# A decoder block on one core: the experts' tokens in half blocks of 64, two with different weights in one product

## The chip, the cores and the metric

The kernel runs on one core of a Trainium2 chip. The metric is the device time of one execution in microseconds (us), here the median of three runs. TensorE is called PE (PEld is its weight load), VectorE DVE, ScalarE ACT, GpSimd POOL and SyncE SP; a name with a q behind it (SPq, PEldq) is the sequencer of that engine, which issues DMAs and works on registers.

## What is computed

A decoder block with pre-normalisation on 4 x 1024 tokens of width 256: causal linear attention with 16 heads, cross attention to 77 context tokens, and a feed-forward part. The feed-forward part is what the change is in:

```python
x1 = x @ sw1.T + sb1;  x2 = x @ sw2.T + sb2            # shared, every token
sh = ln(silu(x1) * x2, s_ln_g, s_ln_b)
shared_out = sh @ sw3.T + sb3
x_moe = x[index_b, index_t]                            # 512 of the 4096 tokens
top1_idx = argmax(sigmoid(x_moe @ eg_w.T + eg_b) + exp_bias)   # one of 8 experts
weights = softmax([shared_score, top1_score])
h1 = x_moe @ ew1[e].T + eb1[e];  h2 = x_moe @ ew2[e].T + eb2[e]
z = ln(silu(h1) * h2, sel_ln_g, sel_ln_b)
expert_out = z @ ew3[e].T + eb3[e]
out[index_b, index_t] = shared_out * weights[0] + expert_out * weights[1]
```

All three parts are added to their input. Everything is float32.

## The kernel before

A tile is 128 tokens; there are 32. Attention and cross attention run as a software pipeline over the tiles (`step(i)` on each engine). Then comes a pipeline over units, in the order of `UNITS`: six groups of four tiles for the shared feed-forward (F0 to F5), G0 (the 512 gathered tokens, for the shared part and for the choice of experts), F6, F7, and the experts' units M0, M1 and M2. Each engine has a loop over q (from 3 to the number of units, or one more) and does in step q its share of units q - 2 to q + 2: `to_features` transposes a unit's input on PE, `gate_products` makes its two hidden products, `z_features` transposes the hidden values, `y_products` makes the output, `gated` and `y_evict` are DVE's parts, `evict_features` and `evict_z` ACT's. Every engine takes its instructions strictly in the order written, so a unit's place in these loops sets what waits behind what. On PE step q = 8 ends with `y_products(7)` (of F6, unit 7) and `to_features(9)` (of M0, unit 9); step 9 is then `z_features(8)`, `gate_products(9)`, `to_features(10)`, `y_products(8)`; step 10 the first half of `gate_products(10)`, `z_features(9)`, the second half, and so on.

The experts' path works as follows. DVE picks each gathered token's expert and its rank among that expert's tokens (`choose_experts`, `choose_slots`). The tokens of an expert are laid out in blocks of 128 slots, each expert starting a new block; there can be at most 4 + 8 - 1 = 11 blocks (`NBLK`), most of them partly empty. POOL scatters the normalised tokens to their slots in DRAM (line 1761, four indirect DMAs). SP waits for them (`placed`) and loads the blocks back (`hs_in`, line 475, one DMA for each M unit of four blocks, the last of three). PE waits for them in `to_features` (`hs_loaded`). `map_blocks` on DVE finds each block's expert. PE reads that number from SBUF into a register (`load_expert`, line 882), and the register picks the weights `we_12` and `we_3` of a block's products from the tiles that hold all eight experts (lines 753 and 803). The bias comes in by one more product with `block_hot` (lines 755 and 806). Meanwhile POOL scatters the rest of each token's result, its weight and its row number to the same slots (line 1735), and SP loads them as `res` (line 467). After the experts' layer norm (POOL finds one over the square root, `m_r`, line 1672), POOL scatters each block's 128 rows to the output, one indirect DMA for each block (line 1746); rows of empty slots fall outside the bounds. In its step q POOL does `scatter_blocks(q - 2)` first and `invert_blocks(q)` last.

SP's part around the change, in its order: for each unit, in `UNITS` order, `store_out` of an F unit waits for DVE's `y_evict` of that unit and stores it; on reaching G0 it waits for `placed` and issues the loads of `hs_in`; on reaching F7 it issues the first `load_base`.

Of the kernel before, what the change touches and what calls it, by code (L numbers as in the profile page):

```python
# [39 lines left out]
NBLK = MT + NE - 1  # L40
# [21 lines left out]
def decoder_block(nc, A):  # L62
    ctx = ExitStack()
    with ctx:  # L64
# [143 lines left out]
        hs_in = wide_[:, 0:2816].rearrange("p (b d) -> p b d", b=NBLK)  # L208
# [3 lines left out]
        m_th, m_u, m_z = (wide_[:, n:n + 512].rearrange("p (j n) -> p j n", j=GT) for n in (9792, 10304, 10816))  # L212

# [5 lines left out]
        iota12 = sb("iota12", [P, 12])  # L219
        iota128 = sb("iota128", [P, MT])  # L220
        over = sb("over", [P, NE, MT])
# [7 lines left out]
        past = sb("past", [P, NBLK, NE])  # L229
        block_e = sb("block_e", [P, 12])  # L230
        block_i = sb("block_i", [P, 12], I32)
        block_oh = sb("block_oh", [BIAS_ROWS, NBLK, NE])
        block_sum = sb("block_sum", [BIAS_ROWS, 12])
        block_hot = sb("block_hot", [BIAS_ROWS, 12], BF16)
# [80 lines left out]
        scattered = sem("scattered")  # L315

# [22 lines left out]
        def is_tile(t):  # L339
            return 0 <= t < NT  # L340

# [50 lines left out]
        def _(sp):  # L392
# [94 lines left out]
        def _(pe):  # L487
# [242 lines left out]
            def gate_products(pe, n, half, expert=None, load_expert=None):  # L730
# [15 lines left out]
                else:  # L746
                    k = UNITS[n][1]
                    for j in range(2 * half, min(2 * half + 2, size(n))):
                        b = GT * k + j
                        dst = sbank[2 + half][:, (j % 2) * D:(j % 2 + 1) * D]  # L750
                        for ch in range(CH):
                            w = we_12[:, bass.ds(expert[b], 1), ch, :].rearrange("p o n -> p (o n)")
                            pe.matmul(dst, h3t[:, n % 2, ch, j * P:(j + 1) * P], w, start=(ch == 0), stop=False)  # L753

                        mm = pe.matmul(dst, block_hot[:, b:b + 1].to_broadcast([BIAS_ROWS, P]), be_16[:, 0:2 * HF],  # L755
                                       start=False, stop=True)
                        if j + 1 < size(n):
                            load_expert()
# [23 lines left out]
            def y_products(pe, n, expert=None, load_expert=None):  # L782
# [10 lines left out]
                for j in range(size(n)):  # L793

                    if is_moe(n) and j % 2 == 0:
                        wait(pe, ys_ready, GT * UNITS[n][1] - 2 + j)
                    if is_dense(n):
                        w = w_3c[:, :]
                    else:
                        wait(pe, mzt_ready, UNITS[n][1] + 1 + (j >= parts(n)[0][1]))  # L800
                        w = we_3[:, bass.ds(expert[GT * UNITS[n][1] + j], 1), :].rearrange("p o n -> p (o n)")
                    dst = bank[1 + j // 2][:, (j % 2) * D:(j % 2 + 1) * D]
                    mm = pe.matmul(dst, z_t[:, n % 2, j * P:(j + 1) * P], w, start=True, stop=is_dense(n))  # L803
                    if is_moe(n):
                        b = GT * UNITS[n][1] + j
                        mm = pe.matmul(dst, block_hot[:, b:b + 1].to_broadcast([BIAS_ROWS, P]), be_16[:, 2 * HF:2 * HF + D],
                                       start=False, stop=True)
# [71 lines left out]
            def load_expert():  # L879
                b = len(expert)  # L880
                if b < NBLK:
                    expert.append(pe.value_load(block_i[0:1, b:b + 1], min_val=0, max_val=NE - 1))
# [218 lines left out]
        def _(dve):  # L1101
# [258 lines left out]
            def expert_constants():  # L1360
# [4 lines left out]
                dve.tensor_tensor_scan(iota12[:, :], zero1[:, 0:1].to_broadcast([P, 12]),  # L1365
                                       one1[:, 0:1].to_broadcast([P, 12]), -1.0, ALU.add, ALU.add).then_inc(cols_ready, 1)
# [3 lines left out]
                dve.tensor_scalar(iota128[:, :], iota12[:, 0:MT], float(P), None, ALU.mult).then_inc(cols_ready, 1)  # L1370
# [56 lines left out]
            def choose_slots():  # L1427
# [3 lines left out]
                then_wait(dve.tensor_tensor(over[:, :, :], total.unsqueeze(2).to_broadcast([P, NE, MT]),  # L1431
                                            iota128[:, :].unsqueeze(1).to_broadcast([P, NE, MT]), ALU.is_gt))
# [4 lines left out]
                then_wait(dve.tensor_scalar(base[:, :], base[:, :], float(P), float(NT * P - 1), ALU.mult, ALU.add))  # L1437
# [11 lines left out]
            def map_blocks():  # L1449
                then_wait(dve.tensor_tensor(past[:, :, :], iota12[:, 0:NBLK].unsqueeze(2).to_broadcast([P, NBLK, NE]),  # L1450
                                            end_block[:, :].unsqueeze(1).to_broadcast([P, NBLK, NE]), ALU.is_ge))
                then_wait(dve.tensor_reduce(block_e[:, 0:NBLK], past[:, :, :], mybir.AxisListType.X, ALU.add))
                then_wait(dve.tensor_scalar(block_e[:, 0:NBLK], block_e[:, 0:NBLK], float(NE - 1), None, ALU.min))
                then_wait(dve.tensor_copy(block_i[:, 0:NBLK], block_e[:, 0:NBLK]))
                rows = slice(0, BIAS_ROWS)
                then_wait(dve.tensor_tensor(block_oh[:, :, :], iota8[rows, :].unsqueeze(1).to_broadcast([BIAS_ROWS, NBLK, NE]),
# [383 lines left out]
```

## Time and profile before

| | |
|---|---|
| time, median of 3 runs | 381.24 us (380.94 to 381.77) |
| the profiled execution's own time | 381.03 us |
| its span, first to last instruction | 379.1 us |
| PE busy | 360.7 us (95%) |
| PE weight load busy | 261.5 us (69%) |
| DVE busy | 298.8 us (79%) |
| POOL busy | 282.3 us (74%) |
| ACT busy | 164.3 us (43%) |

The share of busy time is over the whole span; the change touches only what runs from about 330 us on. Times of instructions are counted from the start of the span.

### The profile page before, as it was taken

The page shows a single profiled execution, that of the slowest core. Times are in us where ns is not written, and L with a number is a line of the kernel's source. Part 1 is how long each engine was busy: PE and PEld are TensorE (multiplying, and loading weights), DVE is VectorE, ACT ScalarE, POOL GpSimd, SP SyncE. Part 2 cuts the span into 40 slices and gives each one's busy share as a digit, 9 for nine tenths or more (in the row PEclk, how much of TensorE's full clock was granted, in tenths as well). Part 3 has the DMA queues.
Part 4 walks back from the last instruction along what each step waited for, and adds up shares of the span by engine and source line. Part 5 has one row for each costly group of instructions (what it writes and reads, how often), then busy time and mean ns, then how long its engine had stood idle before and what let it go on. Part 6 is the DMA issues. An engine that isn't in the chain of part 4 may idle for free. (4 is left out here: it accounts for less than half of the span.)

```text
span 379.1 us, 10587 instructions
## 1 busy us (share of the span) xinstructions
PE 360.7 (95%) x3483; PEld 261.5 (69%) x3483; DVE 298.8 (79%) x934; ACT 164.3 (43%) x395; POOL 282.3 (74%) x417
## 2 busy tenths in 40 slices
PE   8999999999999999999999999999899989998971
PEld 4566677777777777767777777778676566656751
DVE  2588788898989898888898878886756598799771
ACT  1553553453455356436436524432456445341320
POOL 5338987766777866877867789898888888687385
PEclk9999999999999999999999999999999999999997
DMA  8994891300300120032221012003000223136630
GB/s 256 315 310 94 238 298 22 68 16 16 72 30 16 35 54 16 19 83 90 94 52 37 29 24 65 16 22 80 15 30 28 83 86 111 57 115 216 189 109 13
DMA packets 38076, 33.32 MB, mean 88 GB/s; under 512 B 4425, under 2 KB 37224, under 8 KB 38024
## 3 DMA queue, kind: packets, MB, share of 16 engines
q1 hardware_dynamic: 35016, 28.37, 26.4%
q0 software_dynamic: 1456, 3.37, 3.0%
q10 hardware_dynamic: 1552, 0.92, 0.9%
q8 instruction: 29, 0.48, 0.5%
q14 instruction: 23, 0.19, 0.2%
HBM read 15.58 MB, written 13.78 MB: 77 GB/s over the span
## 5 line engine op out<-in xcount | busy, mean ns | idle before, releaser
L1595 POOL TENSOR_TENSOR s_t<-s_t,causal 128x512 f32<-128x512 f32 x63 | 78.9, 1272 | 15.6 <-ACT s_t L909 15.4
L501 PE MATMUL bank<-h1t,w_qkv 128*128 128x512 f32 x112 | 52.9, 595 | 0.4 <-DVE x L1168 0.3
L1155 DVE TENSOR_TENSOR s_t<-sbank,causal 128x512 f32<-128x512 f32 x65 | 43.5, 671 | 1.1 <-PE sbank L522 1.0
L1587 POOL TENSOR_TENSOR state_wide<-state,own_pair 128x256 f32<-128x256 f32 x28 | 18.9, 675 | 25.5 <-DVE state L1146 24.4
L909 ACT ACTIVATE s_t<-sbank 128x512 f32<-128x512 f32 x63 | 33.7, 587 | 7.8 <-PE sbank L522 7.8
L522 PE MATMUL sbank<-arena 32*128 32x256 f32 x512 | 36.7, 400 | 0.0
L561 PE MATMUL bank<-s_t,vp 128*32 128x128 f32 x1024 | 34.6, 275 | 1.1 <-DVE s_t L1155 0.4
L508 PE MATMUL bank<-w_qkv,h1t 128*128 128x256 f32 x128 | 34.2, 389 | 0.0
L1603 POOL TENSOR_TENSOR rr<-ve,neg_half 128x3 f32<-128x3 f32 x36 | 31.9, 887 | 3.0
L646 PE MATMUL bank<-w_out,attn_t 128*128 128x256 f32 x128 | 33.6, 385 | 0.5 <-DVE attn_t L1236 0.5
L740 PE MATMUL sbank<-h1t,w 128*128 128x512 f32 x72 | 33.0, 596 | 0.5 <-ACT h1t L909 0.5
L1190 DVE BATCH_NORM_STATS2 stats<-x 128x6 f32<-128x256 f32 x87 | 31.6, 412 | 0.0
L1112 DVE TENSOR_SCALAR arena<-bank,b_qk 128x512 f32<-128x512 f32 x28 | 21.0, 751 | 13.1 <-PE bank L501 13.1
L909 ACT ACTIVATE prob_t<-bank 77x128 f32<-77x128 f32 x32 | 8.7, 273 | 50.2 <-PE bank L489 50.2
L561 PEld LDWEIGHTS bank<-s_t,vp 128*32 128x32 f32 x1024 | 26.2, 109 | 6.2 <-issue 2.1
L489 PEld LDWEIGHTS bank<-ident,h 128*128 128x128 f32 x128 | 17.6, 140 | 17.3 <-issue 12.4
L501 PEld LDWEIGHTS bank<-h1t,w_qkv 128*128 128x128 f32 x112 | 19.1, 190 | 14.2 <-issue 13.4
L968 ACT ACTIVATE prob<-sc,nmx 128x77 f32<-128x77 f32 x32 | 11.5, 360 | 37.9 <-DVE nmx L1220 37.9
L1614 POOL TENSOR_TENSOR x<-x,b_out 128x256 f32<-128x256 f32 x32 | 26.0, 813 | 0.0
L522 PEld LDWEIGHTS sbank<-arena 32*128 32x128 f32 x512 | 23.1, 184 | 3.9 <-issue 2.4
L646 PEld LDWEIGHTS bank<-w_out,attn_t 128*128 128x128 f32 x128 | 21.8, 190 | 3.5 <-DVE attn_t L1236 1.5
L489 PE MATMUL bank<-ident,h 128*128 128x128 f32 x128 | 24.2, 272 | 0.0
(215 smaller groups left out, 831.7 us busy)
## 6 DMA issues: line engine op xcount, KB each, us to landing
rden_t<-rden SPq DMA_DIRECT2D x64, 64.0 KB
rows<-x SPq DMA_DIRECT2D x32, 128.0 KB, 1.9
x<-in_x SPq DMA_DIRECT2D x7, 512.0 KB, 7.9
out<-x SPq DMA_DIRECT2D x7, 512.0 KB, 2.9
we<-in_we SPq DMA_DIRECT2D x1, 2048.0 KB
rows<-empty SPq DMA_DIRECT2D x1, 1419.0 KB, 6.4
rows<-empty SPq DMA_DIRECT2D x1, 1408.0 KB, 7.6
xmask<-in_mask POOLq DMA_DIRECT2D x2, 616.0 KB, 10.8
```

What stands on the lines that cost most here:

```text
L489: return pe.transpose(dst, src, ident[:, :])
L501: mm = pe.matmul(dst[:, :], w_qkv[:, ch, cb * P:(cb + 1) * P], h1t[:, g % 3, ch, :], start=(ch == 0), stop=(ch == CH - 1))
L508: mm = pe.matmul(v_place(t), h1t[:, (t // GT) % 3, ch, tok(t)], w_qkv[:, ch, 2 * D:3 * D], start=(ch == 0), stop=(ch == CH - 1))
L522: mm = pe.matmul(both, kt(slot, ch)[rows, tok(t)], qpair(slot, ch)[rows, :, tok(t)], start=True, stop=True)
L561: mm = pe.matmul(bank[3][32 * r:32 * r + 32, ch * P:(ch + 1) * P], v_of, s_t[:, r, 2 * ch + par, :], start=(first and ch + par == 0), stop ...
L646: mm = pe.matmul(bank[0][:, 0:D], attn_t[:, M % 2, ch, :], w_out[:, ch, :], start=(ch == 0), stop=(ch == CH - 1))
L740: mm = pe.matmul(sbank[2 + half][:, :], w_12[:, ch, half * HF:(half + 1) * HF], h3t[:, n % 2, ch, :], start=(ch == 0), stop=(ch == CH - 1))
L909: return act.activation(dst, src, ACT.Copy)
L1155: dve.tensor_tensor(s_t[:, r, :, :], sbank[r][:, :].rearrange("p (s q) -> p s q", s=4), causal[:, :].unsqueeze(1).to_broadcast([P, 4, P]), ...
L1190: last = dve.bn_stats(stats[:, k, :], x[:, t, :])
L1595: pool.tensor_tensor(s_t[:, r, :, :], s_t[:, r, :, :], causal[:, :].unsqueeze(1).to_broadcast([P, 4, P]), ALU.mult)\
L1603: pool.tensor_tensor(rr[:, i, :], ve[:, i, :], neg_half[:, 0:3], ALU.pow).then_inc(rr_ready, 1)
```

## The change

A block of 128 slots becomes two halves of 64 slots. Each expert starts a new half, so there are at most 8 + 8 - 1 = 15 halves, held in 8 blocks, and the M units become two of four blocks each. The two halves of a block can belong to different experts. Every product of a block is split in two, each with 64 output partitions (tokens), one for the even half and one for the odd half. The even half's weights come as before by register from the resident tiles. The odd half's weights are loaded from DRAM to places of their own (`we_odd`, in tiles that are free by then), seven blocks with two DMAs each, whose source address SP takes from the odd half's expert number, read by `value_load`. SP does this on reaching G0, ahead of its wait for `placed`. DVE does the first half of `map_blocks` right after `choose_slots`, one step earlier, and the rest (`block_rows`) where it was; the small tiles of both grow (16 halves in place of 11 blocks). The core of it:

```diff
-NBLK = MT + NE - 1
+HB = P // 2
+NHALF = 2 * MT + NE - 1
+NBLK = -(-NHALF // 2)
 NMG = -(-NBLK // GT)
...
+        we_odd = [w_flat[:, 0:we_size], w_flat[:, we_size:2 * we_size], vp_flat[:, 0:we_size],
+                  vp_flat[:, we_size:2 * we_size], rden_t[:, :, :].rearrange("p j d -> p (j d)")[:, 0:we_size],
+                  wide_[:, 2048:2048 + we_size], wide_[:, 11328:11328 + we_size]]
+        we_odd.append(we_odd[-1])
...
                 if n == GATHERED:
+                    sp.wait_ge(expert_ready, 1)
+                    for m in range(NMG):
+                        for b in odd_of(m):
+                            e = sp.value_load(block_i[0:1, 2 * b + 1:2 * b + 2], min_val=0, max_val=NE - 1)
+                            sp.dma_start(we_odd[b][:, 0:2 * CH * HF].rearrange("p (c n) -> p c n", c=CH),
+                                         A["we_12"][bass.ds(e, 1), :, :].rearrange("o (c p) n -> p (o c) n", p=P))\
+                                .then_inc(we_odd_in[m], 16)
+                            sp.dma_start(we_odd[b][:, 2 * CH * HF:we_size],
+                                         A["we_3"][bass.ds(e, 1), :, :].rearrange("o p n -> p (o n)"))\
+                                .then_inc(we_odd_in[m], 16)
                     sp.wait_ge(placed, 16 * MT)
                     for m in range(NMG):
                         b = blocks_of(m)
...
+                    if half == 0:
+                        pe.wait_ge(we_odd_in[k], 16 * 2 * len(odd_of(k)))
                     for j in range(2 * half, min(2 * half + 2, size(n))):
                         b = GT * k + j
                         dst = sbank[2 + half][:, (j % 2) * D:(j % 2 + 1) * D]
                         for ch in range(CH):
-                            w = we_12[:, bass.ds(expert[b], 1), ch, :].rearrange("p o n -> p (o n)")
-                            pe.matmul(dst, h3t[:, n % 2, ch, j * P:(j + 1) * P], w, start=(ch == 0), stop=False)
-
-                        mm = pe.matmul(dst, block_hot[:, b:b + 1].to_broadcast([BIAS_ROWS, P]), be_16[:, 0:2 * HF],
-                                       start=False, stop=True)
+                            w = (we_12[:, bass.ds(expert[b], 1), ch, :].rearrange("p o n -> p (o n)"),
+                                 we_odd[b][:, 2 * ch * HF:2 * (ch + 1) * HF])
+                            for o in range(2):
+                                at = slice(j * P + o * HB, j * P + (o + 1) * HB)
+                                pe.matmul(dst[o * HB:(o + 1) * HB, :], h3t[:, n % 2, ch, at], w[o], start=(ch == 0),
+                                          stop=False, skip_group_check=True)
+
+                        for o in range(2):
+                            hot = block_hot[:, 2 * b + o:2 * b + o + 1].to_broadcast([BIAS_ROWS, HB])
+                            mm = pe.matmul(dst[o * HB:(o + 1) * HB, :], hot, be_16[:, 0:2 * HF],
+                                           start=False, stop=True, skip_group_check=True)
...
-                then_wait(dve.tensor_copy(block_i[:, 0:NBLK], block_e[:, 0:NBLK]))
+                dve.tensor_copy(block_i[:, :], block_e[:, :]).then_inc(expert_ready, 1)
+
+            def block_rows():
...
                 if q == GATHERED:
                     choose_slots()
+                    map_blocks()
                 if q == GATHERED + 1:
-                    map_blocks()
+                    block_rows()
                     weigh()
```

`y_products` is split in the same way, with `we_3` and the last third of `we_odd`. A pair of loads for one block is 256 KB and 128 KB.

## Rows read from the trace of the kernel before

**Rows 1.** POOL in order of time (start, us, what), from 360 us on

```profile
360.38 1.01 POOL L1672 TENSOR_TENSOR m_r<-m_ve,neg_half 128x4 f32<-128x4 f32 x1
361.57 1.05 POOL L1746 DMA_INDIRECT out<-arena,token_u  x1 [0.18 <-issue]
...
365.48 0.97 POOL L1746 DMA_INDIRECT out<-arena,token_u  x1 [0.30 <-issue]
...
366.80 0.88 POOL L1672 TENSOR_TENSOR m_r<-m_ve,neg_half 128x3 f32<-128x3 f32 x1
367.88 1.09 POOL L1746 DMA_INDIRECT out<-arena,token_u  x1 [0.20 <-issue]
...
375.67 0.97 POOL L1746 DMA_INDIRECT out<-arena,token_u  x1 [0.31 <-issue]
```

**Rows 2.** DVE in order of time, its last output

```profile
371.00 1.27 DVE L1301 SCALAR_TENSOR_TENSOR arena<-bank,arena 128x256 f32<-128x256 f32 x3 [1.52 <-PE bank L806]
```

**Rows 3.** PE in order of time, M0's transposes to M1's last gate product

```profile
343.60 1.04 PE L489 MATMUL sbank<-ident,arena 128*128 128x128 f32 x8
344.48 0.60 PE L489 MATMUL bank<-ident,s_t 128*128 128x128 f32 x4
345.91 1.13 PE L753 MATMUL sbank<-we,h1t 128*128 x4 [0.83 <-ACT h1t L909]
346.98 1.03 PE L753 MATMUL sbank<-we,h1t 128*128 x4
...
347.96 1.03 PE L753 MATMUL sbank<-we,h1t 128*128 x4
...
357.35 0.27 PE L755 MATMUL sbank<-be,block_hot 72*128 72x256 bf16 x1
```

**Rows 4.** SP's queue in order of time, 334 to 340 us

```profile
334.05 0.37 SPq L462 DMA_DIRECT2D out<-x  x1
339.46 0.92 SPq L475 DMA_DIRECT2D arena<-rows  x2
```

**Rows 5.** The three loads of hs_in (line 475), issue to landing

```profile
DMA to landing us min/median/max: 3.8/4.9/5.4
```

**Rows 6.** DVE in order of time: F5's output, then map_blocks from first to block_i

```profile
332.37 1.65 DVE L1294 SCALAR_TENSOR_TENSOR x<-bank,z_r,x 128x256 f32<-128x256 f32 x4
...
336.46 0.21 DVE L1450 TENSOR_TENSOR past<-iota,end_block 128x88 f32<-128x88 f32 x1
...
337.19 0.17 DVE L1454 CAST block_i<-block_e 128x11 int32<-128x11 f32 x1
```

**Rows 7.** Reading an expert's number, two in a row, 341 to 342.8 us

```profile
L882 PEldq TENSOR_LOAD <-block_i x2: 299/302/304, 341.3 to 342.0; - x2
L882 PEldq FUSED_REGOPS  x2: 146/146/146, 341.7 to 342.4; - x2
```

**Rows 8.** The page's GB/s by slice; SP's issues in time, and by tile (ns min/median/max)

```profile
GB/s 256 315 310 94 238 298 22 68 16 16 72 30 16 35 54 16 19 83 90 94 52 37 29 24 65 16 22 80 15 30 28 83 86 111 57 115 216 189 109 13
...
0.73 0.46 SPq L394 DMA_DIRECT2D arena<-in_w_xk  x1
...
14.71 4.71 SPq L394 DMA_DIRECT2D x<-in_x  x5
...
L458 SPq DMA_DIRECT2D rows<-x x1: 320/320/320, 55.7 to 55.7; - x1
```

**Rows 9.** PE in order of time in the attention's pipeline, products with 32 columns

```profile
204.47 1.08 PE L561 MATMUL bank<-s_t,vp 128*32 128x128 f32 x32
```

**Rows 10.** Windows: length, busy of PE PEld DVE ACT POOL, granted clock, DMA share, GB/s

```profile
373.00:375.00 2.00, 0.00 (x0) 0.00 (x0) 0.00 (x0) 0.00 (x0) 1.58 (x2) 0.98 0.03 1
375.00:379.10 4.10, 0.00 (x0) 0.00 (x0) 0.00 (x0) 0.00 (x0) 1.33 (x2) 0.50 0.02 0
```

**Rows 11.** PE's first products: in order of time; those in 6 to 8 us, ns min/median/max

```profile
0.99 5.80 PE L843 MATMUL sbank<-ones 128*128 128x512 bf16 x14 [0.99 <-POOL ones L1696]
...
L843 PE MATMUL sbank<-ones x3: 381/484/634, 5.7 to 6.4; 128*128 128x512 bf16 x3
```

More of the change, by code:

```diff
@@ L207, in decoder_block @@
         wide_ = arena[:, :, :].rearrange("p s n -> p (s n)")
-        hs_in = wide_[:, 0:2816].rearrange("p (b d) -> p b d", b=NBLK)
+        hs_in = wide_[:, 0:2048].rearrange("p (b d) -> p b d", b=NBLK)
         res = wide_[:, 2816:2816 + NBLK * BW].rearrange("p (b d) -> p b d", b=NBLK)
@@ L218, in decoder_block @@
         one1 = sb("one1", [P, 1])
-        iota12 = sb("iota12", [P, 12])
-        iota128 = sb("iota128", [P, MT])
-        over = sb("over", [P, NE, MT])
+        iota16 = sb("iota16", [P, 2 * NBLK])
+        iota64 = sb("iota64", [P, 2 * MT])
+        over = sb("over", [P, NE, 2 * MT])
         blocks = sb("blocks", [P, NE])
@@ L228, in decoder_block @@
         slot_y = sb("slot_y", [P, MT], U32)
[L229 to L234, printed above, removed]
+        past = sb("past", [P, 2 * NBLK, NE])
+        block_e = sb("block_e", [P, 2 * NBLK])
+        block_i = sb("block_i", [P, 2 * NBLK], I32)
+        block_oh = sb("block_oh", [BIAS_ROWS, 2 * NBLK, NE])
+        block_sum = sb("block_sum", [BIAS_ROWS, 2 * NBLK])
+        block_hot = sb("block_hot", [BIAS_ROWS, 2 * NBLK], BF16)
         m_ve = sb("m_ve", [P, GT])
@@ L315, in decoder_block @@
         scattered = sem("scattered")
+        expert_ready = sem("expert_ready")
+        we_odd_in = [sem(f"we_odd_in{k}") for k in range(NMG)]
         x_v = A["x"].rearrange("(g j p) d -> g p j d", p=P, j=GT)
@@ L340, in is_tile, with odd_of @@
             return 0 <= t < NT
+        def odd_of(k):
+            return [b for b in blocks_of(k) if 2 * b + 1 < NHALF]
         def blocks_of(k):
@@ L796, in y_products @@
                         wait(pe, ys_ready, GT * UNITS[n][1] - 2 + j)
+                    dst = bank[1 + j // 2][:, (j % 2) * D:(j % 2 + 1) * D]
                     if is_dense(n):
-                        w = w_3c[:, :]
+                        mm = pe.matmul(dst, z_t[:, n % 2, j * P:(j + 1) * P], w_3c[:, :], start=True, stop=True)
                     else:
+                        b = GT * UNITS[n][1] + j
                         wait(pe, mzt_ready, UNITS[n][1] + 1 + (j >= parts(n)[0][1]))
[L801 to L807, printed above, removed]
+                        w = (we_3[:, bass.ds(expert[b], 1), :].rearrange("p o n -> p (o n)"),
+                             we_odd[b][:, 2 * CH * HF:we_size])
+                        for o in range(2):
+                            at = slice(j * P + o * HB, j * P + (o + 1) * HB)
+                            pe.matmul(dst[o * HB:(o + 1) * HB, :], z_t[:, n % 2, at], w[o], start=True, stop=False,
+                                      skip_group_check=True)
+                        for o in range(2):
+                            hot = block_hot[:, 2 * b + o:2 * b + o + 1].to_broadcast([BIAS_ROWS, HB])
+                            mm = pe.matmul(dst[o * HB:(o + 1) * HB, :], hot, be_16[:, 2 * HF:2 * HF + D],
+                                           start=False, stop=True, skip_group_check=True)
                     mm.then_inc(y_done, 1)
@@ L881, in load_expert @@
                 if b < NBLK:
-                    expert.append(pe.value_load(block_i[0:1, b:b + 1], min_val=0, max_val=NE - 1))
+                    expert.append(pe.value_load(block_i[0:1, 2 * b:2 * b + 1], min_val=0, max_val=NE - 1))
             for q in range(3, NU + 1):
@@ L1449, in map_blocks @@
             def map_blocks():
[L1450 to L1453, printed above, removed]
[L1454 removed]
+                then_wait(dve.tensor_tensor(past[:, :, :], iota16[:, :].unsqueeze(2).to_broadcast([P, 2 * NBLK, NE]),
+                                            end_block[:, :].unsqueeze(1).to_broadcast([P, 2 * NBLK, NE]), ALU.is_ge))
@@ L1464, in weigh @@
+                then_wait(dve.tensor_reduce(block_sum[:, :], block_oh[:, :, :], mybir.AxisListType.X, ALU.add))
+                dve.tensor_copy(block_hot[:, :], block_sum[:, :]).then_inc(block_ready, 1)
             def weigh():
```

25 lines of the change are left out of this document (14 added, 11 removed).

## The prediction

> **What bounds the kernel now.** The table of busy time says PE, at 95%, but the change is in the last 50 us, so I read these. The chain of waits ends in POOL's output scatters, and POOL's timeline shows why. After M1's `m_r` (ending 361.39) POOL issues M0's four scatters from 361.57 at 1.27 us each, needs 1.43 us from 366.45 to 367.88 for M2's variance, and issues the other seven, the last at 375.67 [rows 1]. The span ends 2.46 us after that one. So from 361.4 on POOL's queue sets the end. What sets 361.4 is PE: its timeline from M0's transposes at 343.60 to M1's last gate product at 357.4 has one gap, 0.83 us, in which ACT empties the transposes [rows 3]; M1's tail behind it (DVE, then POOL's `m_r`) takes four more. What lets M0's transposes begin at 343.60 is, by the trace, PE's own order. But `hs_in` is close: issued at 339.46, its first part landed 3.8 us later, 343.3 [rows 4, 5]. That slack of 0.3 us is what the change leans on.
>
> **What the change takes away.** Three blocks and one unit. With nothing else moved, M1 is the last unit, and POOL scatters 4 + 4 blocks without a variance between: first at 361.57, last at 361.57 + 7 x 1.27 = 370.46, its end at 371.43 and the span's end, 2.46 us behind the last one's 0.97, at 373.9. That is 5.2 us less. M1's results must be there in time. M1's `m_r` comes at 361.4, and the normalising, transposing, evicting and multiplying of a last unit took 4.6 us, from the end of M2's `m_r` at 367.68 to DVE's last output at 372.27 [rows 1, 2]; with four blocks I allow 5, so 366.4, against M1's first scatter at 366.65. It fits, just. PE's work of M2 was in POOL's shade and brings nothing more.
>
> **What the products cost.** A block's gate products took 347.96 - 346.98 = 0.98 us [rows 3], for four passes over 256 columns and one for the bias. Now there are eight passes and two. Run one after another they double. The trace has such split products: 32 passes with 32 output columns each and 128 rows took 1.08 us, 34 ns a pass with the last one's end [rows 9], while a pass of that length alone (a transpose, eight in 0.88 us) takes 110 [rows 3]. Three to four neighbours ran at once, though both passes of one product go to the same columns. Two groups of 64 should then run two at once and a block stay near 0.98. I take +0.3 us over M0's and M1's gate products for what is lost at the changes of shape. The ends are 0 and 8 x 0.98 = 7.8 us.
>
> **What DVE and the move cost.** `map_blocks` up to `block_i` is 337.36 - 336.46 = 0.90 us and now stands ahead of F5's `y_evict` at 332.37. From 11 elements (0.17 us) to 88 (0.21) an instruction grows by 0.04 [rows 6], so the larger tiles, with up to 40 elements more, add at most 0.15 here, and as much again in `block_rows`. F5's output is then ready 1.05 us later, at 335.1 in place of 334.02. F6's hidden values (`gated`) are later by the same and still in time for PE; the added 0.3 us on DVE before F6's output was read would show as 0.1 to 0.3 us on PE at 341.3, but is covered by the wait that comes next. Without that cover it would cost these.
>
> **What SP's queue costs: the main term.** SP reaches G0 only behind F5's store, then at 334.43, now at 335.5. Then seven blocks, each with one read of a register and two DMA issues, and only after these 14 DMAs the wait for `placed` and the loads of `hs_in`. Prices: reading an expert's number took 0.30 + 0.15 us of work, and on PE two in a row started 0.7 us apart [rows 7]; a 256 KB load in two pieces took 0.46 to issue, a plain 128 KB DMA 0.32 [rows 8]. A block costs at least 0.45 + 0.46 + 0.32 = 1.23 us, say 1.25. With gaps, and the address worked out from the register for each of the two DMAs (an operation like the 0.15 one), I take 1.7, so 11.9 us in all: `hs_in` is issued at 347.4, not at 339.46. `placed` is long done by then. Landing 3.8 us later gives 351.2, and M0's transposes, with all of PE's later queue behind them (F7's transposes, M0's gates, F7's output and its store, M1), start 7.6 us later than at 343.60. The upper end is an issue that finds the queue full: between 0.73 and 14.71 us 21 DMAs took SP 14 us, 0.67 each on average [rows 8]. At 0.67 an issue a block costs 2.05 us, `hs_in` goes out at 349.8 and lands, at the longest landing of such a load, 5.4 us [rows 5], at 355.2: 11.6 us late. The lower end, 1.25 a block, is 344.3, landing at 348.1: 4.5 us late. I go by the middle because the demand, 384 KB in 1.7 us, is 231 GB/s, while the slices of the page with the large loads moved up to 315 [rows 8]. The weights themselves are no wait: M0's land before `hs_in`, and M1's are wanted 5 us later.
>
> The trace has the read of the register at 302 to 306 ns. The Trainium skill ("DMA: Bandwidth & Descriptors", Latency and other measured facts) gives about 600 ns as the floor of such a load; by it the seven reads would add some 2.1 us to this term and the time would be 388. This case's rows are below that floor, and I go by them.
>
> **The clock.** In the wait PE stands idle from 343.6 to 351.2. After the last matmul of the kernel before, at about 371.5 (DVE takes the last outputs from 371.00 on [rows 2]), the granted clock stays full until close to 375 and is then 0.50, 1.2 GHz [rows 10]. A wait of 7.6 us is longer than those 3.4. At the start of the kernel, one kind of product still took 634 ns at 5.7 us and then 381 [rows 11], 253 ns apart for 512 columns, which take 427 at 1.2 GHz and 213 at 2.4. PE had been at these since 0.99: the low level lasted about 5 us of work. After the wait, M0's transposes then take 1.76 and not 0.88 us, ACT's eviction is unchanged, and of the gate products the first 2 us run at half pace, 1.0 us lost. Together +1.9 us. The ends are 0 (clock kept) and 4.4 us (low through M0's gates and the next transposes). The Trainium skill ("TensorE: Matmul & The Clock Gate", Why this matters for your kernels) warns that an idle gap between bursts of matmuls brings the low clock back, which speaks against any change that makes PE wait. By that rule the time is 385.8 and without a fall 383.9; the trace's fall after the last matmul agrees with it, and no row shows the clock inside such a gap.
>
> **The sum.** -5.2 (scatters and unit) + 7.6 (`hs_in` late) + 1.9 (clock) + 0.3 (products) = +4.6 us on the span of 379.1, so 383.7. The profiled execution took 381.03, 1.93 more than its span and 0.2 under the median of the runs; +4.6 on the median of 381.24 is 385.8.
>
> **The rivals.** (a) SP's queue is cheap: register read and issues cost their bare work, 1.25 us a block, and the shorter wait, 4.5 us, ends before the clock falls or little after. Then -5.2 + 4.5 + 0.3 = -0.4, or 380.8, and with each 0.1 us less a block another 0.7. It is faster than before once a block costs under 1.3 us with the clock kept, and under 1.0 with the clock lost. For it speaks that issues of plain DMAs took 0.32 to 0.37 [rows 4, 8]; against it that reads stood 0.7 apart on PE. Chance 0.20, of which 0.14 lies more than 0.2% below and 0.06 within 0.2%, about the least that a measurement of this kernel can tell. (b) The weights clog the queue, 2.05 us a block and 11.6 late: -5.2 + 11.6 + 2.0 + 0.3 = +8.7, 390. The start of the kernel speaks for it, the lower demand here against it: 0.10. (c) The products of two halves run one after another, on top of the forecast: +7.8 and 0.8 for the biases, 394. The 34 ns of [rows 9] speak against it: 0.07. (d) The forecast, 1.4 to 2.0 us a block and some loss of clock: 0.63, by itself 382.5 to 389.
>
> **How the numbers follow.** Slower by over 0.2% are (b), (c) and (d), 0.80; faster 0.14; same 0.06. The range takes in (d), (b) and most of (a) above its middle, and leaves out (c) and the low part of (a): 380.0 to 393.0.
>
> **What would show it.** In the profile of the changed kernel: 14 issues and seven register reads on SP from about 335.5, some 1.7 us for each block; `hs_in` issued near 347; PE idle before M0's transposes for about 7 us, released by the DMA; a granted clock under 1 there; gate products with 64 columns at about 0.98 us a block; eight scatters 1.27 us apart with no variance between; the last starts 8.9 us after the first. The prediction is wrong if SP's part is under 9 us, if the transposes do not wait for `hs_in`, or if a block's products take far more than 1 us.

## The result, and the profile of the changed kernel

| | before | after |
|---|---|---|
| median of the runs, us | 381.28 (4 runs, 380.94 to 381.77) | 389.88 (4 runs, 388.52 to 390.50) |
| ratio, 95% interval | | 1.022, 1.019 to 1.025 |
| profiled execution, its span | 381.03, 379.1 | 390.5, 388.5 |

The change makes the kernel 2.2% slower. The forecast was 385.8, the range 380.0 to 393.0. The sign, the place and all but one term came out; the main term was 5 us too small. By the medians the change costs 8.6 us, 4.0 more than the forecast's 4.6. The two profiled spans differ by 9.4 us (the profiled execution of the kernel after is the slowest of its four), and these have to be found.

SP's queue in order of time (start, us, what), of the kernel after, as [rows 4] of the one before:

```profile
325.47 10.66 SPq L479 DMA_DIRECT2D out<-x  x2
337.36 0.21 SPq L493 DMA_DIRECT2D w_qkv<-in_we  x1
338.10 0.71 SPq L496 DMA_DIRECT2D w_qkv<-in_we  x1
...
342.68 0.38 SPq L493 DMA_DIRECT2D vp<-in_we  x1
343.24 0.34 SPq L496 DMA_DIRECT2D vp<-in_we  x1
344.34 0.38 SPq L493 DMA_DIRECT2D rden_t<-in_we  x1
...
348.62 0.40 SPq L496 DMA_DIRECT2D arena<-in_we  x1
349.07 1.03 SPq L502 DMA_DIRECT2D arena<-rows  x2
```

The first row closes two stores, the second of them F5's, at 336.13. Then come the seven pairs of weight loads, and behind them the tokens, `hs_in` (the last row), 9.6 us later than at 339.46. Of the six steps from one block's first load to the next one's, four are 1.66 to 1.69 us and two are 2.0. The first block's register is read in the 1.23 us in front of its load (336.13 to 337.36). All seven blocks, each with its read, take 349.07 - 336.13 = 12.94, or 1.85 each. Inside most blocks the two pieces start 0.56 apart, and 1.10 pass before the next block's first: that is where the register is read. The landing is late as well. For the two loads of line 502, against [rows 5]:

```profile
DMA to landing us min/median/max: 7.1/7.9/8.7
```

PE in order of time, as [rows 3]:

```profile
341.90 2.48 PE L834 MATMUL bank<-w_3c,s_t 128*128 128x256 f32 x8
356.25 1.94 PE L516 MATMUL sbank<-ident,arena 128*128 128x128 f32 x8 [11.88 <-DMA arena<-rows]
...
359.46 0.68 PE L785 MATMUL sbank<-we,h1t 128*64 x1 [0.41 <-ACT h1t L949]
...
362.54 0.38 PE L785 MATMUL sbank<-we,h1t 128*64 x1
362.55 0.38 PE L785 MATMUL sbank<-vp,h1t 128*64 128x256 f32 x1
...
363.52 0.38 PE L785 MATMUL sbank<-we,h1t 128*64 x1
...
364.59 1.09 PE L516 MATMUL sbank<-ident,arena 128*128 128x128 f32 x8
```

The bracket says what ended the idle time before the instruction: 11.88 us for the DMA of the tokens. M0's transposes start at 356.25 and not at 343.60, 12.65 us later, and go at half pace: 359.46 - 356.25 = 3.21 us to the first product, where it was 2.31, and 5.13 us from there to M1's transposes, where full pace gives four blocks at 363.52 - 362.54 = 0.98 each. The granted clock over that stretch (windows: length, busy of PE PEld DVE ACT POOL, clock, DMA share, GB/s):

```profile
346.00:348.00 2.00, 0.00 (x0) 0.00 (x0) 2.00 (x6) 0.00 (x0) 1.81 (x2) 1.00 0.81 236
348.00:350.00 2.00, 0.00 (x0) 0.00 (x0) 1.03 (x3) 0.00 (x0) 1.39 (x3) 0.51 0.82 234
...
360.00:362.00 2.00, 2.00 (x15) 1.20 (x13) 0.25 (x4) 0.00 (x0) 1.23 (x2) 0.58 0.76 237
362.00:364.00 2.00, 2.00 (x24) 1.35 (x22) 0.80 (x2) 0.38 (x1) 0.00 (x0) 1.00 0.03 8
```

PE's last matmul before the gap ends at 344.4; from about 348 the clock is 0.50, 1.2 GHz, and it is back at full only after 361.6, some 5 us after PE resumed. At the end, POOL in order of time, as [rows 1]:

```profile
374.96 1.01 POOL L1715 TENSOR_TENSOR m_r<-m_ve,neg_half 128x4 f32<-128x4 f32 x1
376.14 1.06 POOL L1789 DMA_INDIRECT out<-arena,token_u  x1 [0.18 <-issue]
377.50 0.99 POOL L1789 DMA_INDIRECT out<-arena,token_u  x1 [0.30 <-issue]
...
385.22 0.98 POOL L1789 DMA_INDIRECT out<-arena,token_u  x1 [0.30 <-issue]
```

Eight scatters without a variance between. Counted from the end of M1's `m_r` to the end of the span it takes 388.5 - 375.97 = 12.5 us, where the kernel before took 379.1 - 361.39 = 17.7: the 5.2 us of gain are there. The account: 12.65 (transposes late) + 0.9 (transposes at the low clock) + 1.1 (gate products, 5.13 against 4.0) - 5.2, and -0.1 left over, is +9.4. Of the 12.65, 0.3 us lie ahead of the change's reach: PE starts F5's output products at 328.94 in this execution, and at 328.62 in that of the kernel before.

### The profile page after: what moved, and what is told of

Same layout as the page of the kernel before. It is cut to its first block, busy times and chain, and to the rows that moved or that the text cites. A ratio compares the mean times of both kernels' runs of the same rounds, so it can differ in the third digit from the quotient of the medians.

```text
span 388.5 us, 10638 instructions
## 1 busy us (share of the span) xinstructions
PE 359.4 (92%) x3514; PEld 257.7 (66%) x3514; DVE 295.6 (76%) x917; ACT 162.4 (42%) x390; POOL 278.8 (72%) x412
## 4 chain that ended last, share of the span: by engine, by line
PE 73%; POOL 9%; issue 8%; DVE 3%; SPq 3%; DMA 2%; ACT 1%; POOLq 1%; DVEq 0%; ACTq 0%
PE bank L528 13%; PE sbank L549 8%; PE bank L588 7%; PE bank L535 7%; PE bank L516 7%; PE bank L673 7%; PE bank L624 3%; PE bank L682 3%; PE bank L572 3%; PE sbank L767 3%; PE sbank L785 2%; DMA arena<-rows 2%; PE sbank L528 2%; PE sbank L516 2%; PE sbank L883 2%
```

## The experiments

Two theories. **A, the forecast's:** the loss is SP's issuing time ahead of the tokens' loads, one register read and two issues with computed addresses for each of seven blocks, and what hangs on it (landing, clock). **B:** the weights' bytes cost it: the DMA engines are busy, tokens and weights land late wherever they are issued. A third point is whether the split products are free. Each ratio is to the kernel before, run beside it on the same chip (its medians 380.87 to 381.80). The last three columns are of the one execution that was profiled; it can be off its kernel's median by over 1 us (e_const, e_best, e_first).

| kernel | median us | ratio to before, 95% | profiled one, us | tokens issued | M0's transposes |
|---|---|---|---|---|---|
| after | 389.88 | 1.022 (1.019 to 1.025) | 390.50 | 349.07 | 356.25 |
| e_noload | 378.69 | 0.991 (0.989 to 0.993) | 379.21 | 339.89 | 344.17 |
| e_order | 382.87 | 1.003 (1.002 to 1.005) | 382.94 | 343.02 | 348.95 |
| e_const | 383.95 | 1.006 (1.004 to 1.007) | 382.87 | 343.32 | 349.24 |
| e_warm | 387.54 | 1.015 (1.013 to 1.017) | 387.03 | 348.18 | 354.90 |
| e_eight | 376.00 | 0.985 (0.983 to 0.987) | 375.98 | 339.32 | 343.47 |
| e_split | 383.98 | 1.006 (1.004 to 1.008) | 384.31 | 339.69 | 343.84 |
| e_act | 382.34 | 1.002 (1.000 to 1.003) | 383.15 | 342.07 | 349.34 |
| e_best | 382.31 | 1.001 (0.999 to 1.004) | 383.44 | 342.40 | 349.20 |
| e_first | 382.21 | 1.002 (1.000 to 1.004) | 380.36 | 339.06 | 343.35 |
| e_last | 381.03 | 1.001 (1.000 to 1.003) | 380.97 | 342.69 | 347.52 |
| e_half | 379.58 | 0.994 (0.992 to 0.995) | 379.38 | 339.67 | 343.94 |
| e_two | 380.37 | 0.997 (0.995 to 0.998) | 380.35 | 341.87 | 345.89 |

**e_noload: the change without its loads.** The odd halves use the resident weights of a fixed expert, so their results are not their experts'.

```diff
-                    sp.wait_ge(expert_ready, 1)
-                    for m in range(NMG):
-                        for b in odd_of(m):
...
-                                 we_odd[b][:, 2 * ch * HF:2 * (ch + 1) * HF])
+                                 we_12[:, b, ch, :])
```

> The odd halves take their weights from a resident tile (expert b for block b), so the 14 loads and the seven register reads on SP fall away and nothing else does; the odd halves' results are not their experts'. Theory (all the loss is hs_in coming late behind the weights' loads, with the clock's fall that follows from PE's wait): hs_in is issued near 340 and the whole gain of the dropped unit appears, -5.2 us, plus 0 to 0.3 for the split products: 376.0 to 376.5. Rival (the split products or the moved map_blocks cost something too): 378 or more.

378.69. The loads cost about 11 us of the 389.88, and without them the change wins 3.0 by the medians. That is over 2 us short of what was expected, and in the rival's range (378 or more). PE's transposes start at 344.17, 0.57 late, though the DMA (issued at 339.89) isn't late any more. Half of this was there before: F5's output products start at 328.91 here and at 328.62 in the kernel before. From there to M0's transposes it is 15.26 us (in e_first and e_half too) against 14.98, and these 0.28 us are DVE's larger work, which makes G0's output products wait for F5's output (in e_first `0.24 <-DVE x`, none before). The rest is at ACT, in order of time:

```profile
349.40 0.38 ACT L1064 ACTIVATE arena<-sbank 128x256 f32<-128x256 f32 x1 [3.07 <-PE sbank L778]
353.10 0.38 ACT L1064 ACTIVATE arena<-sbank 128x256 f32<-128x256 f32 x1 [3.31 <-remote]
```

The second row reads the products of M0's last two blocks. By the record PE ended them at 350.60. The program lets ACT wait here for nothing but PE's semaphore behind these products; the profile names no releaser for it (`remote`) and ends the wait at 353.08. More on this at e_split.

**e_order: M1's three loads behind the tokens.**

```diff
+                    load_odd(0)
                     sp.wait_ge(placed, 16 * MT)
                     for m in range(NMG):
                         b = blocks_of(m)
                         sp.dma_start(hs_in[:, b.start:b.stop, :], hs_v[:, b.start:b.stop, :]).then_inc(hs_loaded[m], 16)
+                    load_odd(1)
```

> SP loads M0's four odd experts, then waits for placed and loads hs_in for both units, then loads M1's three. Theory (order in SP's queue): hs_in is issued at about 344, 5 us earlier than in the changed kernel, lands 4 to 5 us later at 348 to 349, and PE's wait is 7 us shorter; 382 to 384. Rival (the traffic of the weights holds hs_in up wherever it stands, since M0's loads are ahead of it all the same): it still lands 7 us after its issue, at 351 or later, and the time is 385 or more.

382.87, as expected by A: tokens issued 6.05 us earlier than in the kernel after, time 7.0 lower (the rest is a shorter landing, 5.8, and less time at the low clock). The same 14 transfers are made; only the place of M1's six in SP's order is changed.

**e_const: the same 14 transfers from fixed addresses, no register read** (the odd weights are those of expert b).

```diff
-                            e = sp.value_load(block_i[0:1, 2 * b + 1:2 * b + 2], ...)
+                            e = b
-                                         A["we_12"][bass.ds(e, 1), :, :]...
+                                         A["we_12"][e:e + 1, :, :]...
```

> SP's seven register reads are left out: block b's odd half takes expert b's weights from DRAM by a fixed address, in the same 14 DMAs of the same size; the odd halves' results are not their experts'. If SP's own time for issuing is what makes hs_in late, it is issued at about 343.2 and not 349.1, and lands 5.9 us earlier: about 384. If the traffic is (the 16 DMA engines moved only 210 to 270 GB/s here, with 2.75 MB of weights and the other transfers), the landing of hs_in moves by only 1 to 3 us, with an issue to landing of 10 us or more: 387 to 389.

383.95. SP's queue (e_const), the fifth block's pair, the sixth's first, and the tokens:

```profile
340.35 0.43 SPq L493 DMA_DIRECT2D rden_t<-in_we  x1
340.83 0.47 SPq L496 DMA_DIRECT2D rden_t<-in_we  x1
341.34 0.43 SPq L493 DMA_DIRECT2D arena<-in_we  x1
...
343.32 0.98 SPq L502 DMA_DIRECT2D arena<-rows  x2
```

0.99 us a block here, and nothing in front of the first, where the kernel after needs 1.23 us from F5's store (end 336.13) to its first weights. From the store's end to the tokens it is 7.87 us against 12.94, so 1.12 a block against 1.85. This is what separates A from B. Windows of e_const, and then the same of the kernel after:

```profile
336.00:340.00 4.00, 4.00 (x13) 2.03 (x12) 3.76 (x20) 1.14 (x3) 3.20 (x5) 1.00 0.93 291
340.00:344.00 4.00, 3.64 (x14) 1.77 (x12) 3.91 (x9) 0.36 (x2) 3.37 (x2) 1.00 1.08 368
```

```profile
336.00:340.00 4.00, 4.00 (x14) 2.35 (x14) 3.68 (x18) 1.17 (x3) 3.46 (x4) 1.00 0.78 244
340.00:344.00 4.00, 3.91 (x15) 2.07 (x14) 3.89 (x8) 1.02 (x3) 3.11 (x2) 1.00 0.87 268
```

Fed faster, the DMA engines moved 368 GB/s; in the kernel after they moved 268, because SP fed them no faster. So the late issue of the tokens there is SP's time, not the engines'. 5.1 us of it are the reads and computed addresses alone. e_const leaves out both, so their shares aren't told apart.

**e_warm: the kernel after with PE kept busy** in its wait, by 52 products of ones into a free bank.

```diff
                 if q == FIRST_M - 1:
+                    pe.wait_ge(rank_read, 1)
+                    for k in range(52):
+                        pe.matmul(bank[3][:, :], ones16[:, :], ones16[:, 0:1].to_broadcast([P, 512]), ...)
                     to_features(pe, q + 1)
```

> The changed kernel with 52 products of 512 bfloat16 columns on PE in its wait for hs_in, into a bank that nobody uses then (about 11 us of work). Theory of the clock: the granted clock stays at full, M0's transposes take 0.9 us and not 1.74, its first gate products are at full pace: 2.0 us less than the changed kernel, 387.9. If the clock costs nothing, no change: 389.9. If the added products run past the landing, up to 1 us more.

387.54, 2.3 less than the kernel after. PE in order of time (e_warm):

```profile
343.38 11.48 PE L943 MATMUL bank<-ones 128*128 128x512 bf16 x52
354.90 1.06 PE L516 MATMUL sbank<-ident,arena 128*128 128x128 f32 x8
```

The transposes take 0.9 again and not 1.74. From the start of M0's transposes to the end of the span it is 385.2 - 354.90 = 30.3 us, against 388.5 - 356.25 = 32.3: this is the price of the clock measured by itself, 2 us, on top of the wait that causes it. The Trainium skill ("TensorE: Matmul & The Clock Gate", Why this matters for your kernels) says that idle gaps between bursts bring the low clock; this case's windows now show it inside such a gap, which no row of before did.

**e_eight: the gain alone.** The kernel before with eight blocks of 128 and two units; these inputs fill seven such blocks, so for these alone nothing is left out.

```diff
-NBLK = MT + NE - 1
+NBLK = 8
```

> The kernel before with room for 8 blocks of 128 in place of 11, so two units of four (these inputs fill seven; an input that needs more than eight would not fit). Nothing else of the change. Theory: the dropped unit alone brings the -5.2 us of the sum, 376.5 where the kernel before is at 381.7. In the run without the weights' loads only 3.0 of it appeared, with ACT idle 3.3 us at M0's second half for a queue that the profile does not name (2.4 us later than PE's release); if that wait belongs to two units as such, it shows here too and the time is about 379.

376.00, 5.6 less: the gain of dropping three blocks and a unit, as the sum had it (5.2), and no product is split. First scatter 361.80, last 370.88.

**e_split: the price of split products alone.** The kernel before, every block's products in two halves of 64 columns, the odd half with a fixed resident expert's weights (so its results are not its expert's).

```diff
+                            for o in range(2):
+                                at = slice(j * P + o * 64, j * P + (o + 1) * 64)
+                                pe.matmul(dst[o * 64:(o + 1) * 64, :], h3t[:, n % 2, ch, at], w[o], ...)
```

> The kernel before with every product of an expert's block split into two of 64 output partitions; the odd half takes a fixed resident expert's weights, so its results are not its expert's. Theory (two neighbours run at once): within 0.3 us of the kernel before, a block's gate products 0.98 us. Rival (one after another): +0.98 us a block on the path to M1's variance, 8 us or more slower.

383.98, 2.3 us more than before where 0.3 was expected. By the record the products are not slower: M0's blocks start at 346.14, 347.17, 348.14 and 349.12, about 0.98 apart, as before, and the granted clock is 1.00 from 343 to 356. ACT, in order of time (e_split, then the kernel before):

```profile
349.48 0.38 ACT L1048 ACTIVATE arena<-sbank 128x256 f32<-128x256 f32 x1 [3.48 <-PE sbank L760]
352.56 0.38 ACT L1048 ACTIVATE arena<-sbank 128x256 f32<-128x256 f32 x1 [2.69 <-remote]
```

```profile
348.16 0.38 ACT L1036 ACTIVATE arena<-sbank 128x256 f32<-128x256 f32 x1 [2.40 <-PE sbank L755]
350.11 0.38 ACT L1036 ACTIVATE arena<-sbank 128x256 f32<-128x256 f32 x1 [1.57 <-PE sbank L755]
```

M0's second half is read at 352.56 and not at 350.11. PE's record ends at 350.27, but ACT's wait for its semaphore at 352.53. The first half is late too: its products end by the record at 348.32, and it is read at 349.48, where the kernel before has 348.13 and 348.16. Since ends of matmuls are modelled, the record doesn't tell whether PE was late or only its signal, and slower products are not excluded. So +2.3 is measured, its place is shown, its cause is open.

**e_act: the tokens' loads on ACT's queue**, so that they pass SP's loads.

```diff
                 gates(q, 0)
+                if q == FIRST_M - 1:
+                    act.wait_ge(placed, 16 * MT)
+                    for m in range(NMG):
+                        b = blocks_of(m)
+                        act.dma_start(hs_in[:, b.start:b.stop, :], hs_v[:, b.start:b.stop, :]).then_inc(hs_loaded[m], 16)
```

> The changed kernel with the two loads of hs_in on ACT's queue (behind its part of F7's gate, where it has nothing to do), all 14 weight loads left on SP. Theory of the order in SP's queue: hs_in is issued near 340.5 and lands by 345; M0's products then wait only for M0's own odd weights, whose last load is issued at 343.3 and lands at about 346.5, where they would begin anyway; PE's wait is under 2 us and the clock stays full: 377.5 to 380, faster than before. Rival (the traffic of 2.75 MB of weights): hs_in lands at 348 or later wherever it is issued, 381 or more.

382.34; A's number was missed and the rival's came out, with the landing at 349.2. Another queue did not bring the tokens back to 339.5: ACT's own work ahead of them ended at 341.32, they were issued at 342.07 and took 7.1 us to land (windows from 340 to 348: 253 and 291 GB/s). How much of the landing is the weights' traffic, this run doesn't tell.

**e_best: on top of that one transfer of 384 KB a block** (the host lays both weights of an expert side by side), M0's four ahead of F5's store, M1's three behind it.

```diff
+                            sp.dma_start(we_odd[b], A["we_o"][bass.ds(e, 1), :, :].rearrange("o p n -> p (o n)"))
...
+                if n == GATHERED - 1:
+                    load_odd(0)
+                if n == GATHERED:
+                    load_odd(1)
```

> As the run with hs_in on ACT's queue, and each odd half's weights in one DMA of 128 pieces of 3 KB (the host lays the same numbers out as one array more), M0's four of them ahead of F5's store. Theory: SP needs 1.1 us a block and not 1.67 and starts 1.5 us earlier, M0's weights have landed by 344; 0.5 to 1.5 us faster than with hs_in on ACT's queue alone: 376.5 to 378.5. If the weights had already stopped mattering there, no difference.

382.31; missed too. SP is done with M0's loads at 339.25 and ACT with its work at 340.94, and yet the tokens go out only at 342.40, when the slots' scatters have landed (`placed`), and land 6.7 us later. POOL issued the last of these scatters at 337.46, 4.9 us earlier; in the kernel before it was 2.4 (337.05 to 339.46). Here B holds: with SP no longer the limit (336 to 343 GB/s in the windows from 340 to 348), the weights' traffic delays the slots' scatters, and then the tokens. Both theories are right, one after the other. Hence the next runs, in which only the order is changed.

**e_first and e_last: which transfer gives way.** Both with one transfer a block, the tokens on SP.

e_first, behind the two loads of `hs_in`:

```diff
+                    load_odd(0)
+                    load_odd(1)
```

e_last, ahead of F5's store, and behind the two loads of `hs_in`:

```diff
+                if n == GATHERED - 1:
+                    load_odd(0)
...
+                    sp.wait_ge(hs_loaded[1], 16)
+                    load_odd(1)
```

> The kernel after, with SP's order turned round and one transfer a block in place of two: first the wait for the slots and the two loads of the gathered tokens, then all seven register reads and loads of the odd halves. Theory A (what costs is only that the tokens are issued late, by SP's issuing time, and land late under the weights' traffic): tokens issued at 339.9 as without any loads, landed near 345.5; the unit's products must then wait for the fourth block's weights, near 348 instead of 346 to 346.5; that is +2 to +2.5, the clock +0.5 to 1, the dropped scatters -5.2: 378.5 to 380, faster than before. Theory B (the 2.6 MB of weights cost their time wherever they are put, by the DMA engines): no faster than 382, as in the two kernels before. A late release of ScalarE near 350, as in two kernels before, would add 2.3 to either.

> The kernel after with one transfer a block; the first unit's four ahead of the store of F5's output, then the gathered tokens on SP as before, and the second unit's three only when the tokens have landed, so that they meet neither the slots' scatters nor the tokens. Theory A (in the kernel with the tokens on ScalarE's queue it was the second unit's loads that met scatters and tokens and took back the gain): tokens issued at 340 to 341, landing 4.5, TensorE's transposes at 345 to 346 instead of 349.2, clock low for 1 us or less: 378 to 380, faster than before. Theory B (the first unit's four are enough to hold the scatters up): tokens issued after 342 as there, 381 to 382.

382.21 and 381.03, both no different from before by more than 0.2%, which is what B gave; the gain expected from A wasn't there (though e_first met A's times for the tokens, 339.9, and for the first product, near 348), and each shows another place. The ten executions of e_first spread from 379.85 to 382.76, and the profiled one, 380.36, is among the fastest, so its trace shows where time goes but not all of the median. e_first, PE:

```profile
343.35 1.04 PE L514 MATMUL sbank<-ident,arena 128*128 128x128 f32 x8
...
348.51 0.42 PE L783 MATMUL sbank<-we,h1t 128*64 x1 [3.50 <-DMA vp<-in_we_o]
```

The transposes are on time for the first time, and the first product waits 3.50 us for the fourth block's weights: one wait stands ahead of all four blocks. The wait also costs clock: it is 0.50 from 350 to 353, and M0's four blocks take 5.74 us to M1's transposes where e_const's take 4.05. In e_last the weights were there and the tokens late:

```profile
342.69 0.93 SPq L501 DMA_DIRECT2D arena<-rows  x2
...
347.52 1.18 PE L517 MATMUL sbank<-ident,arena 128*128 128x128 f32 x8 [2.43 <-DMA arena<-rows]
```

M0's loads alone, ahead of `placed`, put the tokens 3 us back, as B of this run had it (issued after 342, 381 to 382): SP had nothing left to do from 339.4 on but to wait for `placed`.

**e_half: e_first with the wait split**, a semaphore for M0's first two blocks' weights and one for the other two's.

```diff
+                    if k == 0:
+                        pe.wait_ge(we_odd_in[half], 16 * 2)
+                    elif half == 0:
+                        pe.wait_ge(we_odd_in[2], 16 * len(odd_of(k)))
```

> The kernel with the tokens issued first and one transfer a block, and its wait for the first unit's odd weights split: the first two blocks' products wait for two blocks' weights, the other two's for the other two. There the transposes were on time at 343.35 and the first product waited 3.50 for the fourth block's weights (348.51). Theory A (what is left over is when TensorE first needs each block's weights): products from 346.2, the second half at 348.5, both at full clock or nearly so, the unit's last product ending near 350.7 instead of 354.25: 376.5 to 378 if ScalarE is released on time, 379 to 380 with the release that came 2.3 late near 350 in two kernels. Theory B (the load on the DMA engines costs its time at another place): 380.5 to 382, as there.

379.58, 0.6% faster than before (interval 0.5 to 0.8%): what expectation A gave for the case of a late release. The clock stays at 1.00 from 343 to 356. PE, ACT and POOL of e_half, in order of time:

```profile
347.18 0.42 PE L785 MATMUL sbank<-we,h1t 128*64 x1 [1.56 <-DMA w_qkv<-in_we_o]
```

```profile
352.95 0.66 ACT L1076 ACTIVATE arena<-sbank 128x256 f32<-128x256 f32 x2 [6.85 <-remote]
```

```profile
365.06 1.05 POOL L1789 DMA_INDIRECT out<-arena,token_u  x1 [0.18 <-issue]
...
374.14 0.98 POOL L1789 DMA_INDIRECT out<-arena,token_u  x1 [0.30 <-issue]
```

Of the scatters, the first is 3.5 us later than [rows 1] and the last 1.5 earlier. 1.3 of the 3.5 are PE's start (347.18 against 345.91), and at ACT's read of the second half it is already 3.1 (353.23, the second of the row's two, against 350.11).

**e_two: two of the loads early.** The first two blocks' go ahead of F5's store, the other five stay behind the tokens.

```diff
+                if n == GATHERED - 1:
+                    load_odd([0, 1])
...
-                    load_odd(0)
-                    load_odd(1)
+                    load_odd([2, 3, 4, 5, 6])
```

> The kernel with the split wait, with the first two blocks' odd weights loaded ahead of the store of F5's output, so that behind the tokens only five loads follow. There TensorE waited 1.56 us for the second block's weights (first product at 347.18), and ScalarE's two reads of the first unit's products came together at 352.95, some 3.7 and 0.9 us after the products' recorded ends. Theory A (TensorE's start is what counts): the tokens go out within 0.5 us of 339.7, first product at 346.0 to 346.5, and the time falls by the 0.7 to 1.1 us that the wait is shorter: 378.5 to 379. Theory B (something holds ScalarE's release until about 353 whenever the products end before it, as in three kernels so far, 352.5 to 353.1): the wait disappears, ScalarE reads the second half at about 353 all the same and the time stays at 379.4 to 379.9.

380.37. Neither number: the tokens went out at 341.87, 2.2 later than in e_half, and the transposes at 345.89 waited 2.40 for them. In the window from 336 to 340 the engines moved 357 GB/s (e_first 187, e_last 301, e_best 317): two blocks' weights, F5's store and the slots' scatters together. So theory B of this run wasn't tested: PE came later, and ACT read the second half at 353.95, on time (the first half, whose products end by the record at 351.27, only at 352.37). With none, two and four blocks' weights ahead of `placed` the tokens were issued at 339.1 to 339.7, 341.87 and 342.69. Counted from the issue of the last slots' scatter (e_first and e_half, e_two, e_last) this is 2.4, 5.3 and 5.1 us: two blocks' weights hold the scatters up as much as four.

## Why the prediction was right, and which term was too small

- **What bounds it, and the gain of 5.2.** Right: 5.2 in the profile after, 5.6 in e_eight.
- **The split products, +0.3.** Right in the kernel after: 0.98 us a block. Rival (c), 394, is out: two groups of 64 columns run at once. But as a change by itself the split cost 2.3 us (e_split), by the late release, which the kernel after doesn't show. The forecast knew nothing of that; that the term held in this kernel was in part luck.
- **DVE, +1.05 on F5's output and 0.1 to 0.3 without cover.** F5's output came at 335.74, 0.6 later than worked out, of which 0.3 stood already at 328.9. Without cover it cost PE 0.28 us (e_noload, e_first and e_half), the size that was forecast, but in front of G0's output products and not at 341.3.
- **SP's queue, the main term, 7.6.** The mechanism is right and the size was off: it measured 12.65. The price of a block, 1.7, was near: most steps from block to block were 1.67, but two were 2.0 and the first block took longer, so all seven took 12.94 and not 11.9, 1.85 each. With the 0.6 of F5's output the tokens went out at 349.07 and not at 347.4. The larger error is the landing: 3.8 us was taken from [rows 5], where the tokens' loads meet little else, and it measured 7.1 with 14 weight loads ahead and F6's store behind. The range's upper end had 5.4. So +1.7 and +3.3, together the 5 us that were missing. What made the landing that long is not settled (see the last section).
- **The clock, +1.9.** Right: 2.0 in the account, 2.3 in e_warm.
- **"The weights themselves are no wait."** True of the kernel after, because the tokens were so late. As soon as they weren't, it was wrong: 3.50 us in e_first.
- **Rivals.** (a), 380.8, fell with the price of a block. (b), 390, has the right time by the wrong step: SP took 1.85 us a block and not 2.05, and the rest is the landing, 7.1 against its 5.4. Nor was it the weights' traffic that held SP: e_const issued the same transfers in 7.9 us instead of 12.9. In e_best, e_last and e_two the traffic did come in: it held up the slots' scatters, and with them the tokens.
- **The Trainium skill's floor of about 600 ns for a register load** ("DMA: Bandwidth & Descriptors", Latency and other measured facts) would have given 388, nearer to the result, but not by its reason. SP's seven reads measured, ns min/median/max:

```profile
L492 SPq TENSOR_LOAD <-block_i x7: 58/267/477, 336.2 to 347.3; - x7
L492 SPq FUSED_REGOPS  x7: 152/152/181, 336.7 to 347.6; - x7
```

All are below that floor; without it the seven blocks were priced 1.0 us too low, with it they would have been 1.1 too high.

## What to carry to other kernels

A queue is also an order: what is put ahead of a load that the critical engine waits for costs its issuing time, with register reads and computed addresses 1.85 us a block here where the plain price was 1.12, and its bytes can hold up other transfers that the load waits for. Price both, and take a landing from rows in which the queue is as full as it will be. If large transfers have to be added, first issue what is needed first, then let each consumer wait for its own piece: with one transfer a block in place of two, that took this change from 2.2% slower to 0.6% faster.

## What had not been expected of the hardware

- In three kernels (e_noload, e_split, e_half) ACT's wait for PE's semaphore after M0's products ended 0.9 to 2.5 us after the recorded end of the last one: at 353.08, 352.53 and 352.93, whatever the end (350.60, 350.27, 352.06). The first two blocks' products were read late as well, by 0.8, 1.2 and 3.6 us, and by 1.1 in e_two. In the kernels before, after, e_eight, e_first and e_last both reads came with the ends. The late four have split products between 349 and 353, but so have e_first and e_last, for part of it at the low clock; the granted clock was 1.00 in the late ones at the time. It cost 2.3 us in e_split. The late releases at about 353 all came 0.9 to 1.0 us after POOL had finished the last of its four scatters of the tokens' results, weights and row numbers (352.18, 351.59, 351.97); no run varied that. Whether PE really worked until then, or what held the signal, isn't settled.
- A load of `hs_in`, about 512 KB, took 3.8 us from issue to landing with no weights ahead of it, 3.9 and 4.7 behind two and four blocks' single transfers (e_two, e_last), 5.8 behind M0's eight loads (e_order) or behind all fourteen issued faster (e_const), and 6.7 to 7.1 when issued from ACT's queue or behind all fourteen (e_best, e_act, after), with the engines at 210 to 390 GB/s in these last ones. The amount moved in the meantime doesn't order these cases; what does is open.
- Two matmuls of 64 columns each, with different weights and the same 128 rows, start 10 ns apart and take the time of one, 0.38 us each by the record (362.54 and 362.55).
